# One Silu of a constant column behind the routing exponential of a two-block transformer kernel

## The reference

```python
x = L0_attn_x                                   # (16, 256, 128)
h = _layernorm(x) * (1 + ca) + sa
x = x + ga * _L0_attn_ref(h, ...)               # 16 heads, softmax with relative bias
h = _layernorm(x) * (1 + cb) + sb
x = x + gb * _L0_ffn_ref(h, ...)                # 16 experts, top 4
h = _layernorm(x) * (1 + ca) + sa
x = x + ga * _L1_attn_ref(h, ...)               # sums over time of v * exp(i ...)
h = _layernorm(x) * (1 + cb) + sb
x = x + gb * _L1_ffn_ref(h, ...)

def _L0_ffn_ref(...):
    logits = x @ router_w + router_b
    topv, topi = jax.lax.top_k(logits, K)
    topw = jax.nn.softmax(topv, axis=-1)
    scores = jnp.einsum('tk,tke->te', topw, one_hot)
    gu = jnp.einsum('th,ehf->tef', x, gate_up_proj) + gate_up_bias
    gate = jnp.minimum(gu[..., ::2], LIMIT)
    up = jnp.clip(gu[..., 1::2], -LIMIT, LIMIT)
    glu = gate * jax.nn.sigmoid(gate * ALPHA)
    act = (up + 1.0) * glu
    expert_out = jnp.einsum('tei,eih->teh', act, down_proj) + down_bias
    return jnp.einsum('te,teh->th', scores, expert_out)

def _L1_attn_ref(...):                          # the part with sines
    k = jnp.exp(1j * (k_real * PHASE_SCALE))
    out_pos = _holo_fused_step(v, rotors, jnp.conj(rotors))
    out_assoc = _holo_fused_step(v, jnp.conj(k_shifted), k)
```

## Time and profile before

| | |
|---|---|
| median of 3 runs | 1451.95 us (1451.33 to 1452.53) |
| the profiled execution, its own time | 1452.62 us |
| its span in the profile | 1450.9 us |
| TensorE busy | 1215.8 us, 84% |
| VectorE busy | 1129.5 us, 78% |
| ScalarE busy | 992.0 us, 68% |
| GpSimd busy | 276.6 us, 19% |
| granted TensorE clock, mean | 0.972 of 2.4 GHz |

### The profile page before, as it was taken

One profiled execution on the slowest core, in us unless ns is written; L12 is line 12 of the kernel. 1 busy time (PEld: TensorE's weight loads), 2 busy tenths in 40 slices (PEclk: granted clock), 3 DMA queues, 4 the chain that ended last, 5 costly groups with the idle time before them and its releaser, 6 DMA issues.

```text
span 1450.9 us, 22142 instructions
## 1 busy us (share of the span) xinstructions
PE 1215.8 (84%) x6834; PEld 903.2 (62%) x6834; DVE 1129.5 (78%) x2122; ACT 992.0 (68%) x1716; POOL 276.6 (19%) x260
## 2 busy tenths in 40 slices
PE   3667898888889898888989888898988888798887
PEld 2345575756757575665757566675756667575665
DVE  6435979798897969889796988979697897969765
ACT  1446786867677786767778676777767677776741
POOL 2312130311213120221312022131302113130210
PEclk9979999999999989999998999999899999989998
DMA  5321020303011030301103030210303021020000
GB/s 116 94 25 12 10 26 9 33 8 32 8 17 19 5 33 8 33 8 19 21 5 29 8 33 8 21 19 6 27 8 33 8 23 17 8 25 5 1 5 4
DMA packets 54663, 29.94 MB, mean 21 GB/s; under 512 B 3741, under 2 KB 53610, under 8 KB 54634
## 3 DMA queue, kind: packets, MB, share of 16 engines
q1 hardware_dynamic: 52744, 28.87, 16.1%
q10 hardware_dynamic: 1890, 0.70, 0.5%
HBM read 8.20 MB, written 2.10 MB: 7 GB/s over the span
## 4 chain that ended last, share of the span: by engine, by line
PE 42%; ACT 23%; issue 15%; DVE 14%; DMA 2%; POOL 1%; ACTq 1%; SPq 0%; DVEq 0%; POOLq 0%
PE ring L712 11%; PE pa L726 7%; DVE smax L1722 6%; PE pa L646 4%; PE ring L633 4%; ACT prob L1266 3%; ACT L1299 2%; PE ring L699 2%; PE pb L812 2%; ACT prob L1202 2%; ACT gsc L1255 2%; DVE prod L1827 2%; PE pb_k L742 2%; ACT frac L1302 2%; ACT sin_t L1299 2%
## 5 line engine op out<-in xcount | busy, mean ns | idle before, releaser
L712 PE MATMUL ring<-ht,wgu 128*128 128x256 f32 x1024 | 256.4, 398 | 10.6 <-ACT prob L1266 9.8
L417 POOL TENSOR_TENSOR gsc<-gsc,sc_all 128x512 f32<-128x512 f32 x128 | 167.8, 1316 | 405.2 <-ACT gsc L1260 405.2
L712 PEld LDWEIGHTS ring<-ht,wgu 128*128 128x128 f32 x1024 | 199.9, 199 | 53.9 <-ACT gsc L1255 13.5
L1854 DVE TENSOR_TENSOR_SCAN prod<-keep,prod 128x512 f32<-128x512 f32 x188 | 223.6, 1210 | 0.0
L1787 DVE SCALAR_TENSOR_TENSOR prob<-prob,gsc 128x512 f32<-128x512 f32 x128 | 86.7, 686 | 139.8 <-POOL gsc L417 89.4
L1722 DVE TENSOR_REDUCE smax<-ring 128x4 f32<-128x1024 f32 x128 | 153.0, 1218 | 19.5 <-PE ring L610 16.7
L812 PE MATMUL pb<-prod,wo 128*128 128x256 f32 x544 | 129.3, 382 | 18.9 <-DVE prod L1868 18.9
L1202 ACT ACTIVATE prob<-ring 128x1024 f32<-128x1024 f32 x128 | 125.7, 1023 | 8.7 <-PE ring L633 7.1
L1255 ACT ACTIVATE gsc<-ring,gub_t 128x256 f32<-128x256 f32 x256 | 110.1, 499 | 24.7 <-PE ring L712 24.7
L726 PE MATMUL pa<-prob,wdown 128*128 128x256 f32 x512 | 122.5, 381 | 4.7 <-DVE prob L1787 4.7
L812 PEld LDWEIGHTS pb<-prod,wo 128*128 128x128 f32 x544 | 102.0, 190 | 35.0 <-DVE prod L1868 21.8
(11 more groups left out here) (269 smaller groups left out, 2367.3 us busy)
## 6 DMA issues: line engine op xcount, KB each, us to landing
q_rows<-qk_part SPq DMA_DIRECT2D x144, 64.0 KB
k_rows<-qk_part SPq DMA_DIRECT2D x135, 64.0 KB
x_in<-in_L_attn_x_dram SPq DMA_DIRECT2D x16, 128.0 KB, 2.2
sc_all<-_L_ffn_gate_up_proj_dram SPq DMA_DIRECT2D x1, 2048.0 KB, 12.2
out_dram<-xo SPq DMA_DIRECT2D x16, 128.0 KB, 1.8
prob<-in_L_wmod_dram SPq DMA_DIRECT2D x2, 384.0 KB, 4.1
k_rows<-qk_part ACTq DMA_DIRECT2D x9, 64.0 KB
wo<-in_L_attn_Wo_dram SPq DMA_DIRECT2D x1, 512.0 KB, 7.4
```

The lines of the kernel that those rows point to most:

```text
L417: pool.tensor_tensor(gsc[:, n % NG, :], gsc[:, n % NG, :], sca, ALU.mult).then_inc(S["gsc"], 1)
L712: last = mm(ring[:, n % 2, g * 512 + j * L:g * 512 + (j + 1) * L], lhsT=wgu[:, 2 * n + j, g, :], rhs=ht[:, :], start=True, stop=True, skip ...
L1854: nc.vector.tensor_tensor_scan(prod[:, h, n - 1, :], keep[:, :], prod[:, h, n - 1, :], 0.0, ALU.mult, ALU.add).then_inc(S["cu" + str(n)], 1)
```

## The change

In `route`, one Silu follows the exponential. It reads the constant column `gate_top` (one element on each partition) and writes a new column `silu_set` that nothing reads. It waits for nothing and counts up nothing.

```diff
         gate_top = sb("gate_top", [P, 1])
+        silu_set = sb("silu_set", [P, 1])
         up_top = sb("up_top", [P, 1])
...
                 af(ex[:, :, :], lsh[:, :, :], ACT.Exp).then_inc(S["ex"], 1)
+                af(silu_set[:, :], gate_top[:, 0:1], ACT.Silu)
```

## The result

The changed kernel took 1416.7 us, the median of 4 runs (1416.02 to 1417.79); the kernel before took 1452.2 on the same chip, so the ratio is 0.9755 [0.9738, 0.9772]. The prediction was 1428 (1420 to 1448): right in sign and mechanism, and 11 us too long, 3 us beyond its own range. The profiled execution has a span of 1414.6 us, 36.3 less than before.

The account below looks back on a forecast made before the run. TensorE was taken as the bound, so ScalarE gains only TensorE's waits: 9.8 + 1.3 - 2.3 = 8.8 us off 1452.6 gives 1443.8. Less 15.0 for clock falls gives 1428.8; the median lies 0.65 lower: 1428, range 1420 to 1448.

Parts of the forecast that it names:

- The mechanism: In a step, the load before the sine moves to the added Silu, `bend` finds its table, five loads become four.
- TensorE's whole wait of 0.87 us goes: Expert stage: TensorE's wait for `up` before the fifth pair's products vanishes in each step, at most 9.8 us over the run.
- 0.7 to each lost fall: A step that loses its clock fall gains 4.26 us plus a plain step's 0.7 (0.87 - 0.15), together 5.0 us.
- The Silu at 0.15: Routing stage: the added instruction costs 0.15 us a step (0.10 to 0.24), 2.3 us over fifteen steps.
- The first element, 1.3: First batch element: the load moves into ScalarE's wait for the transposed scores, gaining 1.3 us (1.0 to 2.5).
- Falls of the clock, one for four: Shorter steps break the lock between TensorE's thin stretch and another beat, leaving one fall to 1.2 GHz for four.
- the beat: Something with a period of its own: a fall comes when TensorE's thin stretch meets it, every 252.6 us before the change.
- Some 2 us behind the idle: A clock fall starts 6.57 us behind the routing load, placed some 2 us behind TensorE's idle before line 699.
- sum of 15.0: Gain from one clock fall for four: three steps lose their falls at 5.0 us each, 15.0 us.
- The rule that the monitor runs free: Rival to a fixed number of falls: the clock's monitor does not restart with a kernel, so counts differ by run; no chance given.
- Memory, DMAs and other queues are untouched: Whole kernel: the change affects only ScalarE's instructions and table loads; no gain or cost was priced for memory or transfers.
- The rule on the price of a switch: ScalarE table loads: the skill's 2.66 us a switch against 1.30 us in the trace; by it the sum would be 9.0.

Follow-up runs that it names:

- e6: The changed kernel with 13 one-column Copies in each step ahead of the first `bend`, where the table load was; 1453.29 us, one run.
- e9: The kernel before with two spare products a step in TensorE's idle time ahead of line 699, no other edit; 1436.81 us, ratio 0.9895.
- e7: The changed kernel with ten one-column Copies in each step ahead of attention's second exponential; 1454.49 us, ratio 1.0014 to the kernel before.
- e2: The changed kernel with the Silu in the 15 steps only, not in the first batch element; 1424.36 us, ratio 0.9812 to the kernel before.
- e5: The changed kernel with four one-column Copies in each step ahead of the first `bend`, where the table load was; 1420.87 us, one run.
- e13: The kernel before with the column `silu_set` allocated and no new instruction; 1448.03 us, ratio 0.9984.
- e14: The kernel before with the column `silu_set` allocated and two spare products a step; 1433.85 us, ratio 0.9882.
- e16: e11 without the 16 spare columns, its Exp writing one column allocated last; 1410.28 us, ratio 0.9730 to the kernel before.
- e11: The changed kernel with two spare products a step and a one-column Exp ahead of `route`'s wait for the shifted logits; 1413.53 us, ratio 0.9747.
- e12: e11 with a one-column Silu ahead of the second copy of attention's values in each step; 1420.56 us, ratio 0.9784 to the kernel before.
- e1: The changed kernel with a Copy for the Silu, so the table loads stay where they were; 1457.06 us, ratio 1.0037 to the kernel before.

## Why the prediction was right or wrong

- **The mechanism: right.** The load left `bend`, 16 stand at the Silu and 15 at `tables`, TensorE's wait for `up` went from 9.8 to nothing, and no other wait took its place. e6 shows the cause: ScalarE late again at `bend` brings the wait and the longer step back. A plain step is 81.75, where the prediction had 82.1.
- **"TensorE's whole wait of 0.87 us goes", summed as 9.8: the step that failed.** This term of the sum was mis-sized twice. The 9.8 us of the page is a sum in which the four steps with a fall count almost nothing, so it is no ceiling once the falls are gone; e9 shows 13.1 at full clock. And the listed idle is not the whole cost of a wait: by starts it was 1.12 a step, 0.25 more than the row says. 15 x 1.12 = 16.8 stands in place of 9.8. I had charged 0.7 to each lost fall, which covers 2.1 us of the difference; the other 4.9 are the largest part of the miss, the start's 3.9 the next.
- **The Silu at 0.15: a little dear.** It cost 0.09, just below my lower end of 0.10, 15 x 0.09 = 1.4 us in place of 2.3.
- **The first element, 1.3: right** (1.1).
- **Falls of the clock, one for four: right**, and what the runs can show of the reason is right too: lengthening the step brings them back every third step (e7), and the kernels with steps of 81.74 to 81.81 have one each (the change, e2, e5). What the beat belongs to stays open, and all counts are of single profiles. "Some 2 us behind the idle" was loose: by the earlier trace rows the idle ends 5.21 us behind the routing load and the fall starts at 6.57, 1.4 us later. The one left was a short one, 1.57 us for the 4.26 that I allowed. My sum of 15.0 held three plain gains of 0.7; without them it is 12.8, measured 15.5. The rule that the monitor runs free (the Trainium skill, TensorE: Matmul & The Clock Gate, Part 1) was set down as a rival. The prediction set it aside because three runs of before lay within 1.2 us; 19 later runs of before on one chip lie between 1447.7 and 1456.1, so the narrow spread of the three was chance. The rival has its part: the ten runs of e13 spread over 9.4 us (1443.89 to 1453.33), and those of the kernels with spare products over 0.8 (e14) to 6.1 (e16).
- **"Memory, DMAs and other queues are untouched": wrong.** The column moves every tensor behind it, and 3.9 us of the profile's gain lie at the start, 3.1 of them between the issue of the spread transfers and their first use. The prediction put this term at nothing. No row of before could have priced it, but the sentence left it out of the range as well.
- **Sum in the profile's terms:** 16.8 - 1.4 + 1.1 + 15.5 + 3.9 = 35.9, measured 36.3. Forecast: 9.8 - 2.3 + 1.3 + 15.0 = 23.8.
- **The rule on the price of a switch.** The Trainium skill (ScalarE: Activation LUTs, What ACT_TABLE_LOAD costs) has 2.66 us; here a load and the next start lie 1.29 us apart (579.22, 580.51), and the trace does not agree. (The 1.30 of the prediction can be read in the earlier trace rows, 595.02 - 593.72; the earlier trace rows has only the load.) In the steps nothing hung on it, for TensorE could use 1.12 of the 1.28.
- **The range** ended at 1420 because it took the idle figure of the profile's page for a bound. With 1.12 for a wait and no fall, the lower end would have been near 1452.6 - 16.8 + 1.4 - 1.1 - 17.0 = 1419, and only with the start near 1415.

## What to carry to other kernels

Read the price of a wait from the starts of the instructions around it at full clock, not from its idle figure, and never from a sum over stretches at different clocks. Where the clock falls with a fixed period, look for the idle stretch just ahead of a fall: filling it with products that nobody reads, or changing the step's length by about 1%, can be worth as much as the edit itself (14.4 us from e9's two products, 15.5 from the shorter steps). A function table can be loaded early by an instruction on one column (0.1 us), but the load of 1.28 us needs a place where ScalarE waits or where nobody waits for it: ahead of a wait of 0.90 us it gained 0.44 a step (e11), ahead of one of 0.76 it lost 0.47 (e12). And an added tensor moves those behind it: put it last, or give both kernels the same layout, before their times are compared.

## What I had not expected of the hardware

- An activation of one column has a row of 0.20 us but takes 0.09 to 0.10 us of ScalarE's pace; a Copy in its place also 0.08 a step (e1).
- One added Copy, 0.08 us a step, made the kernel 0.4% slower, by its profile through the clock (11 falls for 4 in the slowest run). Ten Copies on the changed kernel cost it 38 us in all, some 22 of them through falls (five of 4.7 for one of 1.6).
- Falls differ in length from run to run and kernel to kernel, and cost 1.5 to 4.7 us of a step.
- 32 bytes of displacement in SBUF went with 3.1 us between the issue of the first spread transfers and their first use (20.0 to 20.4 us for 23.1 to 23.3, in ten profiles and three); the cause is open.
